# Three matrix exponentials in step: one signal and one predicated copy for each round of squarings

## The chip, the core and the metric

The kernel runs on one core of one Trainium2 chip. The engines of the core are TensorE (PE: matmuls, with PEld for its weight loads), VectorE (DVE), ScalarE (ACT), GpSimd (POOL) and SyncE (SP, which only issues transfers here). The metric is the device time of one execution in microseconds (us); lower is better. Engines run their own instruction streams in order and wait for one another on semaphores.

## What is computed

The reference is a macaron block over x of 8 x 512 x 128: half a feed-forward layer, attention with 16 heads, and half of the same feed-forward layer again. The feed-forward layer normalises x, computes a dense branch, sends each row to 2 of 8 experts, and rotates the expert output by the exponentials of three 128 x 128 generators:

```python
for i in range(NROT):                       # NROT = 3
    moe_out = moe_out @ expm(gens[i])
combined = jnp.concatenate([abel_out, moe_out], axis=-1)
gate = jax.nn.sigmoid(combined @ gc_w + gc_b)
mixed = abel_out * (1.0 - gate) + moe_out * gate
```

## The kernel before

The kernel has no scheduler: each engine's program is written out by hand in the order in which it runs, and semaphores are waited for by value. It has four stages. In the opening stage (to about 149 us of the profile) the rows of all 8 batches ("chunks", numbered n or g) are normalised and routed, POOL scatters them to their experts' regions in DRAM, and beside it the weights are prepared. Then come the experts of the first layer, the attention of 8 batches, and the experts of the second layer.

The weight preparation is where the change lies. The product of the three exponentials is multiplied into the experts' second weights once (`w2_rot`), so the first expert matmul waits for it (`w_ready`). Each exponential is a Taylor series of a scaled generator, squared up to SQUARINGS = 18 times. All 18 rounds are always run. `mats` holds for each generator r the matrix and its transpose side by side (`exp_m`, `exp_T`, 2 x 128 columns). In round i PE makes both squares of each generator into a PSUM bank of that generator, `banks[r]`, and DVE copies them over the matrices where the mask `over[:, r, i]` is set. The semaphore `square_pe` counts PE's finished generators and `squared` counts DVE's finished copies, so before the change PE may square generator 0 of the next round while DVE still copies generators 1 and 2.

The rounds are spread over the routing of chunks n = 2 to 7, three to a chunk; the text calls them A, B and C.

- On DVE, for each n: `gate_logits` (L1633) and `gate_top` (L1645 to L1661, ends with the tile `chosen`), copies of round A, `gate_place` (L1670 to L1685), `gate_shift` (L1628), copies of rounds B and C. After C of n = 2 stands `small_parts` (L1456), after C of n = 3 `make_table` (L1722 to L1751).
- On PE, for each n: `transpose_z(n+1)` (L2197), squares A (L2125 and L2126), `ranks(n)` (L2226 to L2231, which waits for `chosen`), squares B, `abel_logits(n+1)` (L2213 and L2214), squares C, `transpose_w2` (L2112; L2118 for n = 6).
- For n = 7 there are no `abel_logits` and no transposes, so A, B and C are parted by `ranks` alone.

After the last round `fold_rotation` multiplies the three exponentials together (L2132, L2134), makes the rotated weights (L2136, 16 products at L2143) and copies them to `w2_rot` on DVE (L1578). The experts' first PE instruction stands at L2246.

The function `mm` is PE's matmul. An fp32 matmul appears in the profile as two passes, and so does its weight load.

Of the kernel before, what the change touches and what calls it, by code (L numbers as in the profile page):

```python
# [12 lines left out]
U32 = mybir.dt.uint32  # L13
# [5 lines left out]
P = 128  # L19
# [10 lines left out]
NROT = 3  # L30
# [4 lines left out]
SQUARINGS = 18  # L35
# [141 lines left out]
def macaron_block(nc, x, q_w, q_b, k_w, k_b, v_w, v_b, o_w, o_b, ln_gamma, ln_beta, abel_w, abel_b,  # L177
# [11 lines left out]
    with ctx:  # L189
# [3 lines left out]
        def bank(name, shape=(P, 512), dt=FP32):  # L193
            return ctx.enter_context(nc.psum_tensor(name, list(shape), dt))

        def sem(name):
            return ctx.enter_context(nc.semaphore(name))
# [72 lines left out]
        def piece(*shape):  # L270

            n = int(np.prod(shape))
            ap = arena[:, taken[0]:taken[0] + n]
            taken[0] += n
            assert taken[0] <= 2 * NQ * PT_W
            if len(shape) == 2:
                return ap.rearrange("p (a b) -> p a b", a=shape[0])
            if len(shape) == 3:
                return ap.rearrange("p (a b c) -> p a b c", a=shape[0], b=shape[1])
            return ap  # L280
# [7 lines left out]
        mats = piece(NROT, 2, P)  # L288
        exp_m, exp_T = mats[:, :, 0, :], mats[:, :, 1, :]
# [7 lines left out]
        over, shrink = (piece(NROT, SQUARINGS) for _ in range(2))  # L297
# [89 lines left out]


        pair = bank("pair", (P, 2, 512))
        banks = [bank(f"bank{i}") for i in range(6)] + [pair[:, 0, :], pair[:, 1, :]]  # L390

        ps_x, ps_up, ps_y = banks[2:4], banks[0:2], banks[4:6]

# [32 lines left out]
        horner, squared = sem("horner"), sem("squared")  # L426
# [4 lines left out]
        square_pe = sem("square_pe")  # L431
# [87 lines left out]
        def wait(engine, steps, item, step=None):  # L519
            engine.wait_ge(steps.sem, steps.value(item, step))  # L520
# [875 lines left out]
        def _(dve):  # L1396
            v = nc.vector
# [152 lines left out]
            def keep_squares(rounds):  # L1550

                for i in rounds:
                    for r in range(NROT):
                        dve.wait_ge(square_pe, NROT * i + r + 1)
                        v.copy_predicated(mats[:, r, :, :], over[:, r, i:i + 1].bitcast(U32).unsqueeze(2)
                                          .to_broadcast([P, 2, P]),
                                          banks[r][:, 0:2 * P].rearrange("p (a n) -> p a n", a=2)).then_inc(squared, 1)

            def fold_rotation():
                dve.wait_ge(rot_pe, 1)  # L1560
# [341 lines left out]
            for n in range(2, CH):  # L1902
                gate_logits(n)
                gate_top(n)
                keep_squares(range(3 * n - 6, 3 * n - 5))
                gate_place(n)
                if n + 2 < CH:
                    gate_shift(n + 2)
                keep_squares(range(3 * n - 5, 3 * n - 3))
                if n == 2:  # L1910
                    small_parts()
                if n == 3:
                    make_table(0)
# [142 lines left out]
        def _(pe):  # L2056
            mm = nc.tensor.matmul
# [61 lines left out]

            def square(rounds):  # L2120
                for i in rounds:
                    for r in range(NROT):

                        pe.wait_ge(squared, NROT * (i - 1) + r + 2 if i else 1)
                        mm(banks[r][:, 0:P], exp_T[:, r, :], exp_m[:, r, :], start=True, stop=True)  # L2125
                        mm(banks[r][:, P:2 * P], exp_m[:, r, :], exp_T[:, r, :], start=True,  # L2126
                           stop=True).then_inc(square_pe, 1)

            def fold_rotation():
                pe.wait_ge(squared, 1 + NROT * SQUARINGS)  # L2130
                pe.wait_ge(w2T_ok, 5)
                mm(banks[3][:, 0:P], exp_T[:, 1, :], exp_m[:, 2, :], start=True, stop=True).then_inc(rot_pe, 1)  # L2132
                pe.wait_ge(rot_ok, 1)
                mm(banks[3][:, P:2 * P], exp_T[:, 0, :], rot[:, 0, :], start=True, stop=True).then_inc(rot_pe, 1)  # L2134
                pe.wait_ge(rot_ok, 2)
                mm(banks[3][:, 2 * P:2 * P + ROW], b2_T, rot_x, start=True, stop=True).then_inc(rot_pe, 1)  # L2136
                wait(pe, xn_ok, CH - 1)
                wait(pe, placed, CH - 1, 5)
                for q in range(6):
                    if q == 3:  # L2140
                        pe.wait_ge(bias_parts, 1)
                    for i in range(3 * q, min(3 * q + 3, E * NJ)):
                        last = mm(banks[q][:, ROW * (i - 3 * q):ROW * (i - 3 * q + 1)], w2_T[:, i // NJ, i % NJ, :], rot_x,  # L2143
                                  start=True, stop=True)
                    last.then_inc(rot_pe, 1)
# [185 lines left out]
            for n in range(2, CH):  # L2331
                if n + 1 < CH:
                    transpose_z(n + 1)
                square(range(3 * n - 6, 3 * n - 5))
                ranks(n)
                square(range(3 * n - 5, 3 * n - 4))
                if n + 1 < CH:
                    abel_logits(n + 1)
                square(range(3 * n - 4, 3 * n - 3))
                if n - 2 < E // 2:  # L2340
                    transpose_w2(n - 2)
                if n == 6:
                    transpose_b2()
            fold_rotation()

            def scores_for_max(b, u, n):
# [266 lines left out]
```

## Time and profile before

| what | value |
|---|---|
| time, median of 3 executions | 788.86 us (786.06 to 794.77) |
| profiled execution, first to last instruction | 883.8 us |
| mean granted TensorE clock in it | 0.913 of full |
| granted clock from 60 to 150 us of it | 0.78 of full |
| PE busy, DVE busy over the span | 77%, 64% |

The only time of the profiled execution that is at hand is its span, 883.8 us, which is 94.9 us over the median of the executions without a profile. Positions such as "at 91.4 us" are counted from the first instruction of the profiled execution. A row of the timeline gives start, length, engine, line, operation, destination<-sources, shape, count, and in brackets how long the engine had been idle and what ended that; "remote" there, and "another core or an unknown queue" in the chain of waits, mean that no releasing instruction is seen at the end of the wait.

### The profile page before, as it was taken

How to read it: one execution, taken by the hardware profiler on the slowest of the kernel's cores; microseconds unless marked ns; L12 is line 12 of the kernel's file. 1: busy time of each engine (PE TensorE's matmuls, PEld its weight loads, DVE VectorE, ACT ScalarE, POOL GpSimd, SP SyncE). 2: the span in 40 equal slices, each digit the busy share in tenths (PEclk: the TensorE clock that was granted, in tenths of full speed). 3: DMA queues.
4: the chain of work that ended last, by engine and by line, in shares of the span. 5: the costliest groups of instructions: out<-in, count | busy, mean ns of one | idle time of the engine just before them, and what ended most of it. 6: DMA issues, size and time to landing. Idle time of an engine off the chain costs nothing.

```text
span 883.8 us, 16149 instructions
## 1 busy us (share of the span) xinstructions
PE 683.1 (77%) x4719; PEld 492.3 (56%) x4719; DVE 568.2 (64%) x1922; ACT 410.8 (46%) x931; POOL 485.6 (55%) x588
## 2 busy tenths in 40 slices
PE   1465667979897798997988979999997777838760
PEld 1355656979793354654646545455544466837750
DVE  3675545968767876876767767787673235745538
ACT  2243411545560265664545645556554655615530
POOL 2656554034512666576866768373645466566661
PEclk9968777988898899998999999999997999969985
DMA  8614544744348313023050240302201235233525
GB/s 242 205 48 117 132 123 115 183 112 105 94 113 192 110 31 98 18 65 87 2 130 21 49 103 1 98 17 55 61 13 53 85 78 167 75 93 84 175 96 154
DMA packets 89825, 84.04 MB, mean 95 GB/s; under 512 B 14561, under 2 KB 72556, under 8 KB 89580
## 3 DMA queue, kind: packets, MB, share of 16 engines
q1 hardware_dynamic: 74472, 57.51, 25.8%
q0 software_dynamic: 8800, 19.72, 7.5%
q10 hardware_dynamic: 6468, 5.79, 2.8%
q8 instruction: 40, 0.66, 0.3%
q14 instruction: 45, 0.37, 0.1%
HBM read 43.84 MB, written 31.13 MB: 85 GB/s over the span
## 4 chain that ended last, share of the span: by engine, by line
PE 46%; DVE 15%; another core or an unknown queue 11%; issue 7%; ACT 7%; SPq 5%; ACTq 3%; DMA 3%; POOL 1%; DVEq 0%; POOLq 0%
PE bank L2361 6%; PE bank L2271 6%; PE bank L2401 6%; PE bank L2286 6%; PE bank L2426 6%; SPq L595 4%; DVE mx_of L1923 3%; PE pair L2449 2%; PE bank L2363 2%; ACT beside_parts L1254 2%; DMA qT<-mT_zero 2%; PE pair L2213 2%; PE bank L2246 1%; ACT arena L1326 1%
## 5 line engine op out<-in xcount | busy, mean ns | idle before, releaser
L1326 ACT ACTIVATE arena<-bank 128x512 f32<-128x512 f32 x320 | 184.0, 599 | 175.2 <-PE bank L2401 147.1
L1923 DVE TENSOR_REDUCE mx_of<-bank 128x4 f32<-128x512 f32 x320 | 204.2, 684 | 81.9 <-PE bank L2361 42.9
L2401 PE MATMUL bank<-qT,kZ 128*128 128x512 f32 (+3 forms) x512 | 156.9, 377 | 19.2 <-ACT arena L1326 12.4
L975 POOL TENSOR_SCALAR_AFFINE_SELECT arena<-arena 128x256 f32<-128x256 f32 (+1 forms) x192 | 95.4, 521 | 123.9 <-ACT arena L1326 122.5
L2361 PE MATMUL bank<-kZ,qT 128*128 128x512 f32 x320 | 148.5, 481 | 15.7 <-DVE mx_of L1923 6.2
L2401 PEld LDWEIGHTS bank<-qT,kZ 128*128 128x128 f32 x512 | 95.7, 197 | 49.2 <-ACT arena L1326 24.1
L868 POOL DMA_INDIRECT z_rows<-beside_kZ,place x80 | 78.7, 984 | 51.5 <-DVE place L1685 29.8
L2361 PEld LDWEIGHTS bank<-kZ,qT 128*128 128x128 f32 x320 | 63.1, 200 | 70.7 <-issue 31.4
L885 POOL DMA_INDIRECT sums<-y_rows,y_place x56 | 54.4, 971 | 84.9 <-DMA y_rows<-arena 70.0
L2426 PE MATMUL bank<-arena,vA 128*9 128x512 f32 (+3 forms) x1024 | 92.4, 440 | 5.2 <-POOL arena L975 2.7
L1254 ACT ACTIVATE beside_parts<-bank,hidden_bias 128x128 f32<-128x128 f32 x160 | 45.5, 381 | 69.6 <-remote 44.0
L2286 PE MATMUL bank<-w_rot,beside_parts 128*128 x320 | 51.2, 297 | 31.7 <-ACT beside_parts L1254 29.0
L1254 ACT ACTIVATE arena<-bank,hidden_bias 128x128 f32<-128x128 f32 x160 | 45.5, 371 | 48.7 <-PE bank L2271 33.4
L1799 DVE TENSOR_SCALAR arena<-bank,arena 128x132 f32<-128x132 f32 x128 | 39.3, 348 | 44.3 <-remote 25.1
L944 POOL DMA_INDIRECT y_rows<-arena x48 | 49.3, 1026 | 31.8 <-DVE arena L1799 20.5
L2286 PEld LDWEIGHTS bank<-w_rot,beside_parts 128*128 128x128 f32 x320 | 43.9, 197 | 36.2 <-issue 35.3
L2286 PE MATMUL bank<-w_rot,arena 128*128 x320 | 50.4, 295 | 7.0 <-issue 5.2
L868 POOL DMA_INDIRECT z_rows<-w,place x48 | 47.0, 979 | 13.4 <-issue 13.4
L2271 PE MATMUL bank<-beside_parts,beside_qT 128*128 128x128 f32 x320 | 46.6, 286 | 8.3 <-issue 5.1
L2363 PE MATMUL bank<-fixed,ident_bf 128*128 128x512 bf16 x128 | 52.5, 410 | 0.0
L2271 PE MATMUL bank<-arena 128*128 128x128 f32 x320 | 47.0, 291 | 3.8 <-DVE arena L1846 2.2
L2286 PEld LDWEIGHTS bank<-w_rot,arena 128*128 128x128 f32 x320 | 44.6, 200 | 9.0 <-issue 8.2
(286 smaller groups left out, 1306.7 us busy)
## 6 DMA issues: line engine op xcount, KB each, us to landing
arena<-z_rows SPq DMA_DIRECT2D x128, 66.0 KB
qT<-parts SPq DMA_DIRECT2D x42, 128.0 KB
kZ<-parts SPq DMA_DIRECT2D x168, 32.0 KB
y_rows<-arena SPq DMA_DIRECT2D x20, 264.0 KB, 3.3
kZ<-bias_k_r SPq DMA_DIRECT2D x8, 512.0 KB
beside_kZ<-y_rows SPq DMA_DIRECT2D x7, 528.0 KB, 3.9
z_rows<-in_spare SPq DMA_DIRECT2D x4, 528.0 KB
z_rows<-in_spare SPq DMA_DIRECT2D x32, 66.0 KB
```

The lines of the kernel that those rows point to most:

```text
L868: g_.indirect_dma_start(z_rows[run], bass.IndirectOffsetOnAxis(place[g % DEEP][:, k, t:t + 1], 0), zz(g)[:, k, t, :], None).then_inc(z_sen ...
L885: g_.indirect_dma_start(terms(0, c)[0][:, t, k, :], None, y_rows[run], bass.IndirectOffsetOnAxis(y_place[:, c, k, t:t + 1], 0)).then_inc(s ...
L975: g_.affine_select(out=cut, in_=cut, compare_op=ALU.is_ge, fill=0.0, base=0, pattern=[[0, 2], [0, blocks], [1, P]], channel_multiplier=-1) ...
L1254: a_(hidden_rows(layer, p)[:, i, j, :], ps_up[p % 2][:, P * n:P * (n + 1)], ACT.Gelu, bias=hidden_bias[:, j, bass.ds(e, 1)]).then_inc(hidd ...
L1326: a_(dst, src, ACT.Exp).then_inc(exp_ok.sem, 1)
L1923: v.tensor_reduce(mx_of[:, queries, :, t, keys], ps_a[n % NA][:, :].rearrange("p (q n) -> p q n", q=NQ), AX.X, ALU.max).then_inc(reduced.s ...
L2271: last = mm(into, tile(w1_e, j), tile(turned_x(layer, q), t), start=True, stop=True)
L2286: mm(into, hidden_rows(layer, p)[:, i, j, :], w2_rot[:, bass.ds(e, 1), j, :].rearrange("p a n -> p (a n)"), start=(j == 0), stop=False)
L2361: last = mm(into, qT[u][:, t, P * queries:P * (queries + 1)], heads, start=True, stop=(queries != keys))
L2363: last = mm(into, ident_bf[:, :], mask_qk[:, :].unsqueeze(1).to_broadcast([P, NQ, P]), start=False, stop=True)
L2401: return mm(outp, kZ[u][:, h, lo:lo + P], qT[u][:, t, lo:SEQ], start=start, stop=True, skip_group_check=(kind != "full"))
L2426: last = mm(ps_o[32 * q:32 * q + HD + 1, kb * P:SEQ], vA[u][:, kb, NG * q + t, :], pT[t % 2][:, q, PT_KB[kb]:PT_KB[kb] + n], start=(kb == ...
```

## The change

The three banks of the generators become one PSUM tensor `trio` of 3 x 512 columns. A round's six products stand in the same order, but PE waits once before them and signals once after the last, and DVE takes all three results with one predicated copy of 128 x 768. The counts that are waited for follow.

```diff
         pair = bank("pair", (P, 2, 512))
-        banks = [bank(f"bank{i}") for i in range(6)] + [pair[:, 0, :], pair[:, 1, :]]
+        trio = bank("trio", (P, NROT, 512))
+        banks = [trio[:, r, :] for r in range(NROT)] + [bank(f"bank{i}") for i in range(NROT, 6)]
+        banks += [pair[:, 0, :], pair[:, 1, :]]
...
                 for i in rounds:
-                    for r in range(NROT):
-                        dve.wait_ge(square_pe, NROT * i + r + 1)
-                        v.copy_predicated(mats[:, r, :, :], over[:, r, i:i + 1].bitcast(U32).unsqueeze(2)
-                                          .to_broadcast([P, 2, P]),
-                                          banks[r][:, 0:2 * P].rearrange("p (a n) -> p a n", a=2)).then_inc(squared, 1)
+                    dve.wait_ge(square_pe, i + 1)
+                    v.copy_predicated(mats.rearrange("p r a n -> p r (a n)"),
+                                      over[:, :, i:i + 1].bitcast(U32).to_broadcast([P, NROT, 2 * P]),
+                                      trio[:, :, 0:2 * P]).then_inc(squared, 1)
...
                 for i in rounds:
+                    pe.wait_ge(squared, i + 1)
                     for r in range(NROT):
-
-                        pe.wait_ge(squared, NROT * (i - 1) + r + 2 if i else 1)
                         mm(banks[r][:, 0:P], exp_T[:, r, :], exp_m[:, r, :], start=True, stop=True)
-                        mm(banks[r][:, P:2 * P], exp_m[:, r, :], exp_T[:, r, :], start=True,
-                           stop=True).then_inc(square_pe, 1)
+                        last = mm(banks[r][:, P:2 * P], exp_m[:, r, :], exp_T[:, r, :], start=True, stop=True)
+                    last.then_inc(square_pe, 1)
 
             def fold_rotation():
-                pe.wait_ge(squared, 1 + NROT * SQUARINGS)
+                pe.wait_ge(squared, 1 + SQUARINGS)
```

On DVE, at the end of the last chunk (n = 7), the rows before the change are these; `x6` are the copies of rounds B and C, and L1561 is the first copy of `fold_rotation`:

```order
L1681 TENSOR_REDUCE place_of<-pick 128x8 [waits placed]
L1685 CAST place<-place_of 128x8 [waits placed]
L1555 COPY_PREDICATED arena<-arena,bank 128x256 [waits square_pe] x6
L1561 COPY oT<-bank 128x128 [waits rot_pe]
L1563 COPY arena<-bank 128x128 [waits rot_pe]
```

and after it these:

```order
L1682 TENSOR_REDUCE place_of<-pick 128x8 [waits placed]
L1686 CAST place<-place_of 128x8 [waits placed]
L1556 COPY_PREDICATED arena<-arena,trio 128x768 [waits square_pe] x2
L1562 COPY oT<-bank 128x128 [waits rot_pe]
L1564 COPY arena<-bank 128x128 [waits rot_pe]
```

Nothing moved past anything; six copies of 256 columns, each with its own wait, became two of 768. Over the whole program DVE's 54 copies become 18.

On PE, where round B of a chunk ends in `abel_logits` of the next one, before the change (L2226 to L2231 are `ranks`):

```order
L2231 MATMUL bank<-chosen,fixed 128x8 x4
L2125 MATMUL bank<-arena 128x128 [waits squared]
L2126 MATMUL bank<-arena 128x128
L2125 MATMUL bank<-arena 128x128 [waits squared]
L2126 MATMUL bank<-arena 128x128
L2125 MATMUL bank<-arena 128x128 [waits squared]
L2126 MATMUL bank<-arena 128x128
L2213 MATMUL pair<-gate_w,work 128x136 [waits abel_biased,routed,xn_ok]
```

and after it:

```order
L2231 MATMUL bank<-chosen,fixed 128x8 x4
L2125 MATMUL trio<-arena 128x128 [waits squared]
L2126 MATMUL trio<-arena 128x128
L2125 MATMUL trio<-arena 128x128
L2126 MATMUL trio<-arena 128x128
L2125 MATMUL trio<-arena 128x128
L2126 MATMUL trio<-arena 128x128
L2213 MATMUL pair<-gate_w,work 128x136 [waits abel_biased,routed,xn_ok]
```

The order of PE's products is the same, and its three waits became one ahead of the first product.

## Rows read from the trace of the kernel before

**Rows 1.** The page: span, and busy time of each engine.

```profile
span 883.8 us, 16149 instructions
PE 683.1 (77%) x4719; PEld 492.3 (56%) x4719; DVE 568.2 (64%) x1922; ACT 410.8 (46%) x931; POOL 485.6 (55%) x588
```

**Rows 2.** Chain of waits, 129 to 150 us: start us, length us, what.

```profile
138.41 0.45 DVE arena L1555
138.91 0.57 PE bank L2132 x2
...
141.60 5.07 PE bank L2143 x32
...
149.06 1.06 PE bank L2246 x5
```

**Rows 3.** Groups by form, 60 to 150 us: busy us, mean ns, idle before.

```profile
L1555 DVE COPY_PREDICATED arena<-arena,bank 128x256 f32<-128x256 uint32 x54 | 22.1, 440 | 30.3 <-remote 13.4 <-PE bank L2126 11.5 <-issue 5.2
L1578 DVE COPY w_rot<-bank 128x396 f32<-128x396 f32 x5 | 2.7, 566 | 2.5 <-issue 1.5 <-PE bank L2143 0.9
...
L2125 PE MATMUL bank<-arena 128*128 128x128 f32 x108 | 27.6, 345 | 15.3 <-DVE arena L1555 10.7 <-issue 4.7
```

**Rows 4.** Timeline of DVE, chunk n = 4 and the start of n = 5.

```profile
90.90 1.10 DVE L1555 COPY_PREDICATED arena<-arena,bank 128x256 f32<-128x256 uint32 x3
...
94.37 0.45 DVE L1555 COPY_PREDICATED arena<-arena,bank 128x256 f32<-128x256 uint32 x1 [0.41 <-issue]
96.43 0.89 DVE L1555 COPY_PREDICATED arena<-arena,bank 128x256 f32<-128x256 uint32 x2 [1.62 <-PE bank L2126]
97.61 0.45 DVE L1555 COPY_PREDICATED arena<-arena,bank 128x256 f32<-128x256 uint32 x1 [0.28 <-PE bank L2126]
97.94 0.18 DVE L1633 COPY logit<-pair 128x32 f32<-128x32 f32 x1
...
100.10 0.19 DVE L1661 TENSOR_TENSOR chosen<-pick_of 128x32 bf16<-128x32 f32 x1
```

**Rows 5.** Timeline of PE, the same chunk.

```profile
91.04 0.21 PE L2226 MATMUL bank<-chosen,fixed 128*128 128x32 bf16 x1 [5.37 <-DVE chosen L1661]
...
91.40 0.80 PE L2125 MATMUL bank<-arena 128*128 128x128 f32 x2
...
93.69 0.63 PE L2126 MATMUL bank<-arena 128*128 128x128 f32 x2
94.12 0.66 PE L2213 MATMUL pair<-gate_w,work 128*128 128x136 f32 x2
...
95.73 0.44 PE L2125 MATMUL bank<-arena 128*128 128x128 f32 x2
...
96.90 0.39 PE L2126 MATMUL bank<-arena 128*128 128x128 f32 x2
```

**Rows 6.** Timeline of DVE: copies that started long after PE's products.

```profile
76.90 1.10 DVE L1555 COPY_PREDICATED arena<-arena,bank 128x256 f32<-128x256 uint32 x3 [4.41 <-remote]
...
104.80 1.10 DVE L1555 COPY_PREDICATED arena<-arena,bank 128x256 f32<-128x256 uint32 x3 [4.51 <-remote]
...
110.83 0.44 DVE L1555 COPY_PREDICATED arena<-arena,bank 128x256 f32<-128x256 uint32 x1 [2.12 <-PE bank L2126]
112.97 0.44 DVE L1555 COPY_PREDICATED arena<-arena,bank 128x256 f32<-128x256 uint32 x1 [1.70 <-PE bank L2126]
...
115.13 0.44 DVE L1555 COPY_PREDICATED arena<-arena,bank 128x256 f32<-128x256 uint32 x1 [1.73 <-PE bank L2126]
...
129.18 0.43 DVE L1555 COPY_PREDICATED arena<-arena,bank 128x256 f32<-128x256 uint32 x1
132.01 0.44 DVE L1555 COPY_PREDICATED arena<-arena,bank 128x256 f32<-128x256 uint32 x1 [2.40 <-remote]
133.48 0.44 DVE L1555 COPY_PREDICATED arena<-arena,bank 128x256 f32<-128x256 uint32 x1 [1.03 <-remote]
```

**Rows 7.** Timeline of DVE, after the last round: a smaller copy from PSUM.

```profile
139.50 0.29 DVE L1561 COPY oT<-bank 128x128 f32<-128x128 f32 x1 [0.65 <-PE bank L2132]
```

**Rows 8.** One stretch: length, busy us of each engine, granted clock, DMA share, GB/s.

```profile
60.00:150.00 90.00, 57.66 (x410) 52.99 (x409) 48.20 (x246) 23.07 (x55) 49.55 (x49) 0.78 0.50 125
```

## The prediction

> **What bounds the kernel now.** I read the page first [rows 1]: PE is busy for 77% of the span and DVE for 64%, so neither sets the time by its sum, and what a change is worth has to be read in its own stage. The squarings all lie between 61 and 139 us. So I took the chain of waits there next [rows 2]. The reader should see one unbroken line: the last predicated copy (138.41 us), 0.04 us later the first product of the fold (138.91), the rotated weights (L2143), their copies to SBUF (L1578), and the experts' first transposes at 149.06 us. Everything after 149 us waits for the squarings to end, and the experts and the attention are long PE-bound stages behind it. I therefore pass a delay or a gain of the last copy to the end one for one.
>
> Third, the groups by form [rows 3]: 54 copies of 440 ns, with 30.3 us of idle time before them, and PE idle for 15.3 us before its squares, 10.7 of them for the copies. Here two engines hand each other work and both wait; neither is saturated. What counts is the length of the round trip, not the number of instructions.
>
> **What a copy costs.** The 54 small copies become 18 of 128 x 768, a form the trace lacks. A copy from PSUM of 128 columns takes 0.29 us [rows 7] and one of 396 takes 0.566 us [rows 3]: 0.276 us for 268 columns, 1.03 ns a column. The predicated copy of 256 takes 0.440 us [rows 3]; 512 columns more add 0.53 us, which makes 0.97 us. Bounds: not under 0.86 us, if only 0.83 ns a column were added, and not over the 1.10 us that three chained small ones take from first start to last end [rows 4]. I take 0.97 us, since the slope comes from the same kind of access. For DVE alone this is a gain of 0.13 us a round where all three products lie ready, 18 x 0.13 = 2.3 us of its time.
>
> **What a hand-over costs.** Before, PE starts the next round when the first generator's copy has ended, 0.44 us after the copies start; now it waits for all three. Likewise the last generator's copy started when its own product was done and ended 0.44 us later; now the 0.97 us copy starts there. Each time the round trip grows by 0.97 - 0.44 = 0.53 us, if PE waits for DVE there and nothing else does the waiting. Chunk n = 4 shows the three kinds [rows 4, 5].
>
> - A to B: the copies start at 90.90 us, with no idle time before them. PE's B starts at 91.40 us, behind the first copy; the new copy ends at 90.90 + 0.97 = 91.87 us, so B starts at about 91.93 us, 0.53 us late. There are 6 of these, one a chunk: 6 x 0.53 = 3.2 us. Queued behind on PE are `abel_logits` and C, which are late by the same.
> - B to C: between them PE has the logits, 94.12 to 95.73 us, 1.6 us. The last copy of B starts at 94.37 us; the new one would start 0.53 us later, at 94.90 us, and end at 95.87 us, while PE, also 0.53 us late, asks for it at 96.26 us. Hidden, with 0.4 us to spare, for n = 2 to 6: cost 0. If that cover were gone each would cost up to 0.53 us, 2.7 us in all.
> - C to the next chunk: DVE's next routing step stands behind the last copy of C in the queue. That copy ran from 97.61 us, and the logits' copy followed at 97.94 us; with B's delay the new copy starts at 98.14 us and the logits' copy follows at about 99.0 us: 1.06 us late, of which 0.53 us is new. PE's A of the next chunk is also late by this, but it runs beside DVE's routing, 2.3 us from the logits' copy to the end of `chosen` at 100.29 us, and it takes 1.4 us at the clock of round C [rows 5]. Who waits is PE's `ranks` and then B, behind `chosen`. 5 times 0.53 = 2.7 us.
> - The last chunk has no logits between B and C and no routing behind C: two more hand-overs with no cover, 1.1 us. There the fold waits at once [rows 2].
>
> The sum is 13 x 0.53 = 6.9 us, with nothing on the other side: the 0.13 us that a finished set of copies saves is spent ahead of `gate_place`, which is off the path while PE's B is later than it. The bank tensor itself costs nothing, since the same banks are used by the same instructions; fewer waits on DVE cost nothing either.
>
> **What the stalls take out of it.** This stage has longer waits than the round trip. At 76.90 and 104.80 us the copies of A began after 4.4 and 4.5 us of idle time that ends in nothing visible; at 110.83, 112.97 and 115.13 us the three copies of one round came 2.1 us apart; and 132.01 and 133.48 us follow 129.18 us in the same way [rows 6]. If such a wait ends at a time that something else sets, a chunk that arrives 1.06 us late loses nothing in front of it. Counting only what lies behind the last stall, the price is three hand-overs of n = 7, 1.6 us; with no stall at all it is 6.9 us. The profiled execution took 95 us more than the median without a profile, so I take its stalls to be longer than in the timed runs but not absent, and stand in the middle: 4.2 us. The sum is made against the profile's own 883.8 us, which would become 888; it lies 94.9 us over the median of 788.86 us, and since the price is in copy durations and not in a share of the span, the same 4.2 us go on the median: **793 us**.
>
> **A rule against the change.** The rows show DVE idle for 30.3 us before these copies [rows 3]. The Trainium skill, page "Perfetto Trace Analysis", section "Optimizing Scalar/DVE Operations", says that grouping into larger operations helps throughput when the engine is saturated, and that where Scalar or Vector are not saturated but cause bubbles elsewhere, breaking instructions up may let work finish sooner. By that rule the change goes the wrong way here, which is the sign that I forecast; read as if DVE were saturated, it would promise 2.3 us of gain instead. The Trainium skill, page "VectorE: DVE Perf Modes", section "The TRN2 errata — SBUF-src ops pay a fixed extra latency per instruction", gives 120 + columns cycles at 0.96 GHz for a VectorE operation from PSUM; my estimate from it is 0.39 us for 256 columns (the trace says 0.44) and 0.93 us for 768, 0.53 us more, and so the same sum.
>
> **Rivals.**
>
> - *The signals are what is slow, and there are fewer of them* (faster). The copies at 110.83, 112.97 and 115.13 us look like a queue of PE's signals that is served one every 2.1 us while transfers are heavy [rows 6]. If each signal pays, one per round comes at the time of the first: 115.13 - 110.83 = 4.3 us gained there and 133.48 - 129.18 = 4.3 us in the last chunk. With the hand-overs paid in full, 6.9 - 8.6 = -1.7 us; if the 4.4 us stalls shrink by half too, -6 us: 783 to 787 us. Against it: at 76.90 and 104.80 us three copies ran back to back after the stall, so there the three signals came at once, and the last is what one signal would wait for.
> - *The clock falls with the added idle time* (slower). PE's 12 passes of a round take 2.7 us in B of n = 4 (91.40 to 94.12) and 1.4 us in C (95.73 to 97.1) [rows 5]: the same passes at 1.2 and at 2.4 GHz, and over the stretch the granted clock is 0.78 [rows 8]. B came after PE had stood idle for 5.4 us waiting for `chosen` [rows 5]. If half a microsecond of more idle time at each hand-over keeps PE at 1.2 GHz for one more round in a chunk, that is 1.3 us x 6 = 8 us on top of up to 6.9 us, 797 to 804 us. It decides from the point where 0.5 us more of idle time suffices. Against it: the long idle times are there already, and C came back to full clock within the same chunk.
> - *The stalls cover everything, or the large copy is nearly as quick as the small one*: no change, 788 to 790 us. For it speaks that 13.4 us of the idle time ends at no visible releaser [rows 3].
> - *The change does not do what it says* can be left aside: the order of instructions shows 18 copies and one wait a round.
>
> **How the numbers follow.** 1% is 7.9 us, about what a measurement of this kernel can tell from no change. The forecast (+1.6 to +6.9 us, 790.5 to 795.8) gets 0.58; no change (788 to 790.5) 0.14; the signals (783 to 787) 0.14, a third of it under 781; the clock (797 to 804) 0.14. Of the forecast's and the no-change case's chance a little goes past the bounds, because the median of three executions itself ranged from 786.06 to 794.77 us. The range of 784 to 800 us leaves out the lower part of the signals' case and the upper part of the clock's. Faster by over 1% (under 781.0): 0.05. Slower by over 1% (over 796.8): 0.14. Within 1%: 0.81.
>
> **What would show it.** In the profile after, the copy of 128 x 768 should take 0.93 to 1.0 us and stand 18 times; PE's B should start about 1.0 us after the copy of A starts; the last copy should end about 1 us before the fold's other steps as now, but later than the products by 0.97 instead of 0.44 us. The experts' first instruction should come 1.6 to 7 us later than at 149.06 us if the stalls stay as they are. Copies that start right after PE's products, with the stalls gone [rows 6], would speak for the signals. A granted clock in 60 to 150 us clearly under 0.78 [rows 8] would speak for the clock. I would be wrong altogether if the stage's length moved by more than 8 us: then the stalls, not the copies, are what the change moves.

## The result, and the profile after

| | before | after |
|---|---|---|
| time, median of 4 executions each, on one chip | 788.52 us (786.06 to 794.77) | 800.37 us (797.14 to 802.89) |
| ratio, with its 95% interval | | 1.0142 (1.0108 to 1.0176) |
| profiled execution | 883.8 us, and 786.2 us in a second one | 795.4 us |

The changed kernel is slower by 1.4%, 11.2 us, with an interval of 8.5 to 13.9 us. The forecast was slower by 4.2 us with bounds of 1.6 to 6.9 us: its direction held and its size did not. The median lies 0.4 us above the upper end of the range that was given (784 to 800 us).

The first thing to settle was what to compare with. The profile of before that the prediction rests on lasted 883.8 us, against 788 us for the executions that were only timed. So the same kernel was profiled once more, and that execution ("the second profile of before" from here on) took 786.2 us. The top of its page answers to [rows 1]:

```profile
span 786.2 us, 16149 instructions
PE 651.7 (83%) x4719; PEld 471.6 (60%) x4719; DVE 565.6 (72%) x1922; ACT 410.9 (52%) x931; POOL 484.8 (62%) x588
```

The page of the changed kernel begins:

```profile
span 795.4 us, 16113 instructions
PE 654.0 (82%) x4719; PEld 473.9 (60%) x4719; DVE 560.5 (70%) x1886; ACT 412.4 (52%) x931; POOL 485.7 (61%) x588
```

DVE has 36 instructions fewer and 5.1 us less work (565.6 to 560.5), and PE's work is the same within 2.3 us. The span is 9.2 us longer. The change takes work from an engine and lengthens the kernel, so the time must be in waits.

The groups by form answer to [rows 3]. In the second profile of before, over 60 to 140 us (busy us, mean ns of one, idle us ahead and what ended it; the first three of its 54 copies lie before 60 us):

```profile
L2125 PE MATMUL bank<-arena 128*128 128x128 f32 x99 | 20.6, 290 | 0.5 <-DVE arena L1555 0.5
L1555 DVE COPY_PREDICATED arena<-arena,bank 128x256 f32<-128x256 uint32 x51 | 20.2, 440 | 5.1 <-PE bank L2126 4.3 <-issue 0.7
```

and in the changed kernel over the same stretch:

```profile
L2125 PE MATMUL trio<-arena 128*128 128x128 f32 x102 | 22.5, 305 | 6.4 <-DVE arena L1556 6.4
...
L1556 DVE COPY_PREDICATED arena<-arena,trio 128x768 f32<-128x768 uint32 x18 | 18.2, 1012 | 17.0 <-PE trio L2126 17.0
```

The reader should see three things. The idle time ahead of the copies, 30.3 us in [rows 3], was 5.1 us in the second profile of the same kernel, and the 13.4 us that ended at "remote" are not there at all: those stalls belonged to one execution. After the change the idle time is 17.0 us, all of it for PE's products, and PE in turn waits 6.4 us for the copies where it waited 0.5 us. And the copy of 768 columns takes 1.012 us, against 0.97 forecast, while three small ones are 0.440 us each and overlap, so that they take 1.10 us from the first start to the last end.

One chunk shows the round trip. This is DVE's timeline for n = 5 in the second profile of before, which answers to [rows 4] (rows with x3 are the three copies of a round):

```profile
84.65 0.18 DVE L1633 COPY logit<-pair 128x32 f32<-128x32 f32 x1
...
86.94 1.10 DVE L1555 COPY_PREDICATED arena<-arena,bank 128x256 f32<-128x256 uint32 x3
...
89.10 1.10 DVE L1555 COPY_PREDICATED arena<-arena,bank 128x256 f32<-128x256 uint32 x3
90.89 1.34 DVE L1555 COPY_PREDICATED arena<-arena,bank 128x256 f32<-128x256 uint32 x3 [0.69 <-PE bank L2126]
92.13 0.18 DVE L1633 COPY logit<-pair 128x32 f32<-128x32 f32 x1
```

The same chunk on DVE after the change:

```profile
90.78 0.18 DVE L1634 COPY logit<-pair 128x32 f32<-128x32 f32 x1
...
93.01 1.00 DVE L1556 COPY_PREDICATED arena<-arena,trio 128x768 f32<-128x768 uint32 x1
95.71 1.03 DVE L1556 COPY_PREDICATED arena<-arena,trio 128x768 f32<-128x768 uint32 x1 [0.51 <-PE trio L2126]
98.44 1.02 DVE L1556 COPY_PREDICATED arena<-arena,trio 128x768 f32<-128x768 uint32 x1 [1.70 <-PE trio L2126]
99.35 0.17 DVE L1634 COPY logit<-pair 128x32 f32<-128x32 f32 x1
```

And PE's first product of round B, before and then after, which answers to [rows 5]:

```profile
87.43 0.49 PE L2125 MATMUL bank<-arena 128*128 128x128 f32 x2
```

```profile
94.07 0.49 PE L2125 MATMUL trio<-arena 128*128 128x128 f32 x2 [0.56 <-DVE arena L1556]
```

From the start of A's copies to the start of B it was 87.43 - 86.94 = 0.49 us and is 94.07 - 93.01 = 1.06 us: 0.57 us more, the difference of the two copies' lengths (1.012 - 0.440). From one logits' copy to the next the chunk took 92.13 - 84.65 = 7.48 us and takes 99.35 - 90.78 = 8.57 us: 1.09 us more, two hand-overs. The copies of C, which in before began as soon as the first generator's products were there and then went on beside PE, now stand idle for 1.70 us until the last product is done.

The same reading for all chunks (from the start of each logits' copy, us):

| chunk | second profile of before | after | more |
|---|---|---|---|
| n = 2 | 8.12 | 9.27 | 1.15 |
| n = 3 | 10.90 | 13.72 | 2.82 |
| n = 4 | 9.28 | 10.35 | 1.07 |
| n = 5 | 7.48 | 8.57 | 1.09 |
| n = 6 | 7.41 | 8.54 | 1.13 |
| n = 7, to the end of the last copy | 7.11 | 8.63 | 1.52 |

Together 8.8 us. Four chunks have two hand-overs' worth (1.14 us), the last has a little less than the three that the sum gives it (1.7 us), and n = 3 has 1.7 us more than its two, which comes back below as the clock.

Then the chain of waits behind the squarings, which answers to [rows 2]. After the change it reads (start us, length us, what):

```profile
124.05 0.79 DVE w_rot L1579 x2
...
124.89 2.50 issue
127.39 0.64 PE trio L2246 x4
```

In [rows 2] the experts' first transposes come last in an unbroken line behind the rotated weights, and in the second profile of before they follow at once: its weights were ready at 115.2 us and this row of PE's timeline follows (L1403 is the helper by which DVE signals `w_ready`):

```profile
115.31 1.09 PE L2246 MATMUL bank<-ident,arena 128*128 128x128 f32 x8 [0.70 <-DVEq L1403]
```

After the change there are 2.5 us in which PE waits, with the weights ready, for something that the chain doesn't name. So the experts' start moves from 115.31 to 127.39 us, by 12.1 us: 1.1 us by which the squarings began later in that execution (59.7 against 58.6 us), 8.8 us in the squarings, -0.2 us between them and the rotated weights, and 2.4 us more of this wait (2.5 against 0.1).

### The profile page after: what moved, and what is told of

Its sections match the earlier page's. It is cut to its first block, busy times and chain, and to the rows that moved or that the text cites. A ratio compares the mean times of both kernels' runs of the same rounds, so it can differ in the third digit from the quotient of the medians.

```text
span 795.4 us, 16113 instructions
## 1 busy us (share of the span) xinstructions
PE 654.0 (82%) x4719; PEld 473.9 (60%) x4719; DVE 560.5 (70%) x1886; ACT 412.4 (52%) x931; POOL 485.7 (61%) x588
## 4 chain that ended last, share of the span: by engine, by line
PE 51%; DVE 21%; issue 7%; DMA 6%; POOL 5%; ACT 4%; ACTq 3%; SPq 3%; DVEq 0%; POOLq 0%
PE bank L2426 8%; PE trio L2271 6%; PE bank L2286 6%; PE trio L2361 5%; DVE mx_of L1924 4%; PE trio L2401 4%; PE bank L2401 3%; PE bank L2361 3%; PE pair L2213 3%; DMA qT<-mT_zero 2%; POOL y_rows L946 2%; SPq L597 2%; PE pair L2449 2%; DVE arena L1556 2%; PE trio L2363 2%
## 5 line engine op out<-in xcount | busy, mean ns | idle before, releaser
L1924 DVE TENSOR_REDUCE mx_of<-trio 128x4 f32<-128x512 f32 x216 | 142.6, 684 | 40.6 <-PE trio L2361 24.1
L1328 ACT ACTIVATE arena<-trio 128x512 f32<-128x512 f32 x170 | 101.0, 600 | 82.8 <-PE trio L2401 81.9
L1328 ACT ACTIVATE arena<-bank 128x512 f32<-128x512 f32 x150 | 89.6, 597 | 72.2 <-PE bank L2401 71.4
L2361 PE MATMUL trio<-kZ,qT 128*128 128x512 f32 x216 | 99.6, 470 | 6.9 <-DMA kZ<-parts 2.2
L1924 DVE TENSOR_REDUCE mx_of<-bank 128x4 f32<-128x512 f32 x104 | 71.2, 684 | 28.6 <-PE bank L2361 27.2
L2401 PE MATMUL trio<-qT,kZ 128*128 128x512 f32 (+3 forms) x272 | 83.2, 372 | 5.2 <-DMA qT<-mT_zero 5.2
L2401 PE MATMUL bank<-qT,kZ 128*128 128x128 f32 (+2 forms) x240 | 73.2, 366 | 1.0 <-ACT arena L1328 0.2
L2401 PEld LDWEIGHTS trio<-qT,kZ 128*128 128x128 f32 x272 | 49.4, 192 | 20.9 <-DMA qT<-mT_zero 7.3
L2361 PE MATMUL bank<-kZ,qT 128*128 128x512 f32 x104 | 49.0, 471 | 7.6 <-DVE mx_of L1924 4.0
L870 POOL DMA_INDIRECT z_rows<-w,place x48 | 46.9, 976 | 13.4 <-issue 13.4
L2401 PEld LDWEIGHTS bank<-qT,kZ 128*128 128x128 f32 x240 | 45.1, 192 | 13.5 <-ACT arena L1328 8.6
```

Of the source, the lines that this page charges most:

```text
L870: g_.indirect_dma_start(z_rows[run], bass.IndirectOffsetOnAxis(place[g % DEEP][:, k, t:t + 1], 0), zz(g)[:, k, t, :], None).then_inc(z_sen ...
L1328: a_(dst, src, ACT.Exp).then_inc(exp_ok.sem, 1)
L1924: v.tensor_reduce(mx_of[:, queries, :, t, keys], ps_a[n % NA][:, :].rearrange("p (q n) -> p q n", q=NQ), AX.X, ALU.max).then_inc(reduced.s ...
L2361: last = mm(into, qT[u][:, t, P * queries:P * (queries + 1)], heads, start=True, stop=(queries != keys))
L2401: return mm(outp, kZ[u][:, h, lo:lo + P], qT[u][:, t, lo:SEQ], start=start, stop=True, skip_group_check=(kind != "full"))
```

## Experiments

All ratios are to the kernel before, from executions on the same chip and with their 95% intervals. One program serves for most kernels. It has the PSUM tensor `trio` and says with two tables which generators' products signal and which copies are joined. Its difference from before, without the two functions that count up to the right semaphore value:

```diff
-        banks = [bank(f"bank{i}") for i in range(6)] + [pair[:, 0, :], pair[:, 1, :]]
+        trio = bank("trio", (P, NROT, 512))
+        banks = [trio[:, r, :] for r in range(NROT)] + [bank(f"bank{i}") for i in range(NROT, 6)]
+        banks += [pair[:, 0, :], pair[:, 1, :]]
...
-                    for r in range(NROT):
-                        dve.wait_ge(square_pe, NROT * i + r + 1)
...
+                    for lo, hi in COPIES[i]:
+                        dve.wait_ge(square_pe, signals_up_to(i, hi))
+                        v.copy_predicated(mats[:, lo:hi, :, :].rearrange("p r a n -> p r (a n)"),
+                                          over[:, lo:hi, i:i + 1].bitcast(U32).to_broadcast([P, hi - lo, 2 * P]),
+                                          trio[:, lo:hi, 0:2 * P]).then_inc(squared, 1)
...
-                        pe.wait_ge(squared, NROT * (i - 1) + r + 2 if i else 1)
+                        pe.wait_ge(squared, copies_up_to(i - 1, r) if i else 1)
...
+                        if r in SIGNALS[i]:
+                            last.then_inc(square_pe, 1)
```

A round that is "joined" has SIGNALS[i] = [2] and COPIES[i] = [(0, 3)]; one that is "apart" has [0, 1, 2] and [(0, 1), (1, 2), (2, 3)]. The results:

| kernel | ratio | interval | squarings, us | weights ready, us | experts' start, us |
|---|---|---|---|---|---|
| second profile of before | | | 48.1 | 115.2 | 115.31 |
| tensor only | 0.9996 | 0.9962 to 1.0030 | 48.2 | 115.9 | 116.01 |
| one signal, small copies | 1.0127 | 1.0091 to 1.0162 | 54.2 | 120.3 | 126.92 |
| three signals, one copy | 1.0160 | 1.0128 to 1.0192 | 55.6 | 123.1 | 126.53 |
| the change | 1.0142 | 1.0108 to 1.0176 | 56.8 | 124.8 | 127.39 |
| before, biases first | 0.9989 | 0.9963 to 1.0014 | 48.2 | 116.2 | 116.31 |
| one signal, small copies, biases first | 1.0068 | 1.0042 to 1.0094 | 54.2 | 120.8 | 121.37 |
| the change, biases first | 1.0090 | 1.0062 to 1.0119 | 56.8 | 125.3 | 125.45 |
| only rounds A joined, biases first | 1.0014 | 0.9984 to 1.0044 | 52.9 | 120.9 | 121.03 |
| only rounds C joined, biases first | 0.9988 | 0.9955 to 1.0022 | 50.3 | 116.5 | 117.09 |
| only the last two joined, biases first | 1.0001 | 0.9964 to 1.0038 | 49.8 | 118.9 | 119.03 |
| only rounds B joined | 0.9981 | 0.9952 to 1.0009 | 48.7 | 116.2 | 116.84 |
| only rounds B joined, biases first | 0.9974 | 0.9946 to 1.0002 | 48.5 | 116.8 | 116.87 |

"Squarings" is from the start of the first predicated copy to the end of the last, in the kernel's profile. There is one profile for each kernel, so these lengths have no interval of their own.

**Before, once more.** No edit. It tells what the stalls of the first profile are.

> The kernel before once more, for a profile that can be compared with the one after: its first one was 95 us over the timed runs. Hand-over theory (each joined round costs the round trip the large copy's 1.01 us in place of 0.44 us, nothing else changes): the span is about 787 us, the copies of round A start right behind the routing, and the last copy ends about 8 us earlier than in the changed kernel, at about 108.5 us from the first instruction. Rival (something behind the squarings pays too, the attention or the experts): the squarings end less than 8 us earlier and the rest of the 11 us lies behind 150 us.

It took 787.93 us, with a span of 786.2 us. The stalls are gone: the squarings take 48.1 us, not the 75.9 us (63.0 to 138.9) of the first profile. So what is in [rows 6] belongs to that one execution. None of the profiles of the other kernels, with spans of 785 to 799 us, has it either.

**The tensor only.** All rounds apart: three signals and three copies, as before, from the one PSUM tensor.

> Only the PSUM tensor over three banks is kept; three signals and three copies of 256 columns a round as before. Hand-over theory: no change, 787 to 790 us. Rival (the joined tensor, or where the banks lie, costs part of the 11 us): 791 to 795 us.

0.9996 (to within 0.3% on each side) and 48.2 us: no cost of the layout or of the rewritten form of the copy can be seen.

**One signal, small copies.** PE waits for each generator's copy by itself but signals once a round.

```diff
+SIGNALS[i] = [2] in all 18 rounds
+COPIES[i] = [(0, 1), (1, 2), (2, 3)] in all 18 rounds
```

> One signal of TensorE a round, but still three copies of 256 columns, each with a wait of TensorE of its own. Hand-over theory: the copies of A still give the first generator free after 0.44 us, so A to B costs nothing; behind a last product DVE now needs 1.10 us in place of 0.44 us, 0.66 us x 5 chunks and once ahead of the fold, and the uncovered hand-over of the last chunk costs 0.8 us: 4.8 us in all, about 793 us. Rival (signals are dear, fewer are better): 785 us or less.

It was slower than expected: 1.0127, 801.6 us. The squarings took 6.0 us more than with the tensor only. A copy of generator 0 can't start until the last product is done. By chunks, n = 3 alone is 2.70 us longer than with the tensor only, where n = 2, 5 and 6 are 0.56 to 0.67 us longer; some 2.0 us of the 6.0 are therefore the fall of the clock that is told below, and 4.0 us are the hand-overs, which is somewhat less than the 4.8 us expected. The other part of the miss is behind the squarings. The chain of waits there:

```profile
117.61 2.69 DVE w_rot L1596 x6
...
120.36 6.56 issue
126.92 1.09 PE trio L2264 x4
```

The weights are ready at 120.3 us and PE starts 6.6 us later.

**Three signals, one copy.** The reverse.

```diff
+SIGNALS[i] = [0, 1, 2] in all 18 rounds
+COPIES[i] = [(0, 3)] in all 18 rounds
```

> Three signals of TensorE a round as before, but one copy of 768 columns that waits for the third, and one wait of TensorE. Hand-over theory: the same as the whole change, 799 to 801 us, since the copy waits for the last product either way. Rival (fewer signals give something back or cost something): it differs from the whole change by more than 2 us.

1.0160: it has as many signals as before and costs as much as the whole change, so the number of signals has no price that can be seen. It must wait for the last product as well, and adds the long copy. Its squarings are 7.4 us longer than with the tensor only (55.6 against 48.2), which is 13 x 0.57; its n = 3 is 1.2 us longer, without the fall of the clock. After this run the wait of 2.5 to 6.6 us behind the ready weights stood in all three slow kernels, and in neither of the others.

**The wait behind the weights.** PE's code ahead of L2246 names three waits: `w_ready`, `expert_bias_in` (the experts' biases) and `w1_in`. The biases are three loads of 2.1 KB that ScalarE issues when `bias_parts` is set, shortly ahead of the rotated weights. The rows of the timeline on the issues in the changed kernel (start us, us from the first to the last, queue):

```profile
115.36 3.29 SPq L609 DMA_DIRECT2D kZ<-bias_k_r  x3
121.17 2.13 ACTq L1270 DMA_DIRECT2D expert_bias<-arena  x3
```

and in the second profile of before:

```profile
110.95 2.13 ACTq L1268 DMA_DIRECT2D expert_bias<-arena  x3
113.21 0.90 SPq L607 DMA_DIRECT2D kZ<-bias_k_r  x2
```

SyncE's loads of the attention's key rows are 512 KB each and are released by POOL's scatters. In before the small loads go ahead of the last two of them; after the change, with the squarings' end 9.9 us later and chunk 6's scatter only some 5 us (from about 113 to 118 us), they go behind. With one signal and small copies the two queues issue at the same time: the large loads at 118.39 and 118.81 us, the small ones at 117.61, 118.44 and 119.14 us. Their packets, in the groups of transfers by queue (packets, MB, share): for one signal with small copies, first in 117 to 123 us, then in 123 to 127 us:

```profile
q10 hardware_dynamic: 29, 0.00, 0.4%
```

```profile
q10 hardware_dynamic: 19, 0.00, 0.4%
```

In the second profile of before, over 110 to 114.5 us:

```profile
q10 hardware_dynamic: 48, 0.01, 1.0%
```

The same 48 packets took 3.4 us from first issue to last landing (110.95 to 114.3 us) in the one and 9.2 us (117.61 to 126.8 us) in the other, and 6.1 us (121.17 to 127.3 us) in the changed kernel. The times of the last of their semaphore's increments in the traces say that this is what PE waits for: 126.83 us with one signal and small copies, 126.44 us with three signals and one copy, 127.30 us in the change, and in each PE starts 0.09 us later (126.92, 126.53, 127.39 us). In the second profile of before the last increment comes at 114.34 us, ahead of the ready weights at 115.2 us. The test is to hold the large loads back until the small ones have landed:

```diff
             for q in range(X_TOP, X_BUFS):
                 load_x(0, q)
+            sp.wait_ge(expert_bias_in, 16 * 3)
             for g in range(5, CH - 1):
                 key_rows_of(g)
```

It was put into the kernel with one signal and small copies, into the change, and into before as a control.

> One signal a round, three copies, and SyncE waits for the three small loads of the experts' bias rows before it issues the key rows of chunks 5 to 7 (512 KB each). Theory of the overtaken loads (the experts start only when these 2.1 KB loads have landed, and they now come behind the key rows): w_rot is ready at about 120.3 us and the experts start there, not at 126.9 us, so 5 to 6 us less than with one signal alone, a ratio to before of about 1.006. Rival (the experts' start waits for something else, the scatter or the x rows): no change, ratio 1.012 to 1.014.

> The whole change with the same wait of SyncE. Overtaken loads: w_rot is ready at 124.8 us and the experts start at about 125 us, where they started at 127.4 us: 2 to 3 us less than the changed kernel, ratio to before 1.011 to 1.012. What is left is the hand-overs, 8 us. Rival: ratio 1.014 to 1.016 as before.

> The kernel before with the same wait of SyncE. Overtaken loads: there the loads land at 114.3 us, ahead of w_rot at 115.2 us, so nothing is gained: ratio 0.998 to 1.002. Rival (key rows issued later free the transfers for all else): faster by over 3 us.

The chain of waits with one signal, small copies and the biases first:

```profile
120.84 0.53 issue
121.37 0.64 PE trio L2265 x4
```

and its issues, now in the other order:

```profile
118.09 2.13 ACTq L1287 DMA_DIRECT2D expert_bias<-arena  x3
...
121.29 1.41 SPq L625 DMA_DIRECT2D kZ<-bias_k_r  x3
```

The wait behind the weights fell from 6.6 to 0.5 us, and the ratio from 1.0127 to 1.0068. The 0.5 us are still the biases, which now land at 121.28 us, 3.2 us after their first issue. In the change it fell from 2.5 to 0.1 us, and the ratio from 1.0142 to 1.0090 (its interval and the earlier one, 1.0062 to 1.0119 and 1.0108 to 1.0176, still touch). Before gains nothing from the same edit (0.9989), since it had no such wait. So the late biases are shown as a cost of the change. The wait that went is 0.3% of the time and the ratios differ by 0.5%, with an uncertainty of nearly as much. 0.9% remain, 7.6 us (796.69 against 789.11 us for before with the same edit). In the profiles of these two kernels the squarings differ by 8.6 us and the experts' start by 9.1 us, so the squarings are the cause to look at for the rest.

**One kind of round at a time.** The prediction has a term for each kind of hand-over, so each kind was joined alone: rounds B of chunks 2 to 6; rounds A of 2 to 7; rounds C of 2 to 6; and B and C of the last chunk, which have no cover.

```diff
+fused B:    SIGNALS[i] = [2], COPIES[i] = [(0, 3)] for i in (1, 4, 7, 10, 13)
+fused A:    the same for i in (0, 3, 6, 9, 12, 15)
+fused C:    the same for i in (2, 5, 8, 11, 14)
+fused last: the same for i in (16, 17)
```

> One signal and one copy only in rounds B of chunks 2 to 6, where the logits stand between B and C on TensorE; all other rounds as before. Hand-over theory: the copy of B is hidden under the logits, the squarings end where they ended before (106.7 us) within 0.5 us, ratio 0.998 to 1.002. Rival (each joined round costs the same, 0.6 us): the squarings end 3 us later, ratio 1.004 or more.

> With the wait of SyncE for the bias rows, one signal and one copy only in the six rounds A; all others as before. Hand-over theory: TensorE's B starts 0.57 us later in each of six chunks, 3.4 us in all: ratio to before 1.003 to 1.006, and the last predicated copy ends about 3.4 us later after its first one than the 48.1 us of the kernel before. Rival (only the last stretch counts): ratio 0.998 to 1.001.

> The same, joined only in rounds C of chunks 2 to 6. Hand-over theory: the last copy of C ends 0.57 us later in five chunks, and the routing behind it: 2.9 us, ratio 1.002 to 1.005, 2.9 us more than 48.1 us from the first copy to the last. Rival (TensorE's early start of the next round A was what mattered, and it hides behind the routing): ratio 0.998 to 1.001.

> The same, joined only in rounds B and C of the last chunk, where nothing stands between them on TensorE. Hand-over theory with what the profile after showed: in its last chunk the rounds came 2.7 us apart where three copies keep up with TensorE at 1.34 us a round, so B to C costs 1.1 us or somewhat less and C to the fold 0.57 us behind a copy of B that waits for the routing: 1.0 to 1.7 us, ratio 1.000 to 1.003. Rival: nothing.

> Joined only in rounds B of chunks 2 to 6, with the wait of SyncE: what the runs so far leave as the best that can be made of the change. Hand-over theory: no difference that can be told, ratio 0.997 to 1.001. Rival (fewer copies on VectorE give something once nobody waits for them): under 0.996.

In the squarings' length, against 48.2 us of before with the biases first: A 4.7 us, C 2.0 us, the last two 1.5 us, B 0.3 us, together 8.5 us, where the whole change adds 8.6 us. That they meet so closely is in part luck, since chunks in which nothing is joined differ by up to 0.5 us as well: n = 4 takes 9.28 us in the second profile of before and 9.70 us in before with the biases first, and of the 1.5 us of the last two only 1.16 us lie in their own chunk. In their own chunks the kinds read so: A costs 0.55 to 0.58 us in n = 2, 4, 5 and 6, nothing in n = 7 as long as B and C behind it are apart, and 2.47 us in n = 3; C costs 0.56 to 0.62 us in n = 2, 3, 5 and 6 and can't be read in n = 4; the last two cost 1.16 us together, two times 0.58. B costs 0.3 us for five with the biases first and 0.5 us without (48.7 against 48.2 us with the tensor only), nearly all of it in n = 4, so close to nothing, as worked out.

The times are another matter: 1.0014, 0.9988, 1.0001 and 0.9974, all with intervals of 0.3 to 0.4% to each side that hold 1. A's stage is 4.7 us longer, its experts start 4.7 us later, and of this 1.1 us of time was measured, with an interval of -1.3 to 3.5 us. So the lower part of what A alone was expected to cost (1.003 to 1.006) is just within the interval, and the one for one that I had counted on is not. Added up, the four ratios give 2 us less than before, with an uncertainty of about 5 us (my estimate from their intervals), where the whole change with the biases first is 7 us slower. The lengths of the parts add up to the whole and their times do not; no run explains that. The kernel with only B joined and the biases first has the lowest ratio, by medians 790.85 against 791.83 us, and can't be told from before.

## Why the prediction was right or wrong

**The bound was right.** The last copy, the fold, the rotated weights and the experts' start are one line in every kernel. They did not move as one block. From the end of the last copy to the ready weights nine profiles, both kinds of before among them, take 8.3 to 8.5 us at a mean granted clock of 0.79 or 0.80, and four (the two with one signal and small copies, C joined, and B joined without the biases first) take 7.0 us at 1.00. And the experts' biases can come later than the weights.

**The copy was sized nearly right**: 1.012 us against 0.97, so a hand-over costs 0.57 us and not 0.53. That makes the full sum 13 x 0.57 = 7.4 us in place of 6.9. The slope is (1.012 - 0.440) / 512 = 1.12 ns a column; for the 0.83 ns of the lower bound no row stood. The estimate from the Trainium skill, page "VectorE: DVE Perf Modes", section "The TRN2 errata — SBUF-src ops pay a fixed extra latency per instruction", 0.93 us, was further off.

**The count of hand-overs was right,** but for A of n = 7, which costs nothing by itself. A and C cost 1.07 to 1.15 us a chunk in four chunks of five, two times 0.57 and nearly nothing else, and B to C was hidden behind `abel_logits`: 0.3 to 0.5 us for five of them where uncovered ones would have cost 2.9. In the changed kernel's n = 5, B's copy ended at 96.74 us and PE asked for it at 96.83 us, so the spare is about 0.1 us, where 0.4 us was forecast from n = 4 at another clock. The last chunk's three came to 1.5 us, against 3 x 0.57 = 1.7.

**The step that failed is the halving for the stalls.** I took the full sum down from 6.9 to 4.2 us because waits of 2 to 4.5 us stood in [rows 6], and argued that they were "longer than in the timed runs but not absent". They were absent. The profiled execution was 95 us longer than the timed ones, and the second profile of the same kernel has a span within 3 us of the timed median and 5.1 us of idle time ahead of the copies. The full sum, which stood in the text as the upper bound, is what the squarings pay: 7.4 us of the 8.8 us measured, with 1.7 us of the clock beside it and 0.3 us less than the sum in the other chunks. The prediction had said that a stage longer by more than 8 us would mean that the stalls are what the change moves. The stage is 8.8 us longer, and there were no stalls to move: that sign would have misled.

**The clock happened in one place.** The rival put the loss of 1.3 us into every chunk. It came in n = 3 alone. The stretch of n = 3's round B, after the change (length, busy us of PE, PEld, DVE, ACT and POOL, granted clock, DMA share, GB/s):

```profile
70.00:74.00 4.00, 3.99 (x20) 3.84 (x21) 2.00 (x10) 2.87 (x8) 3.08 (x4) 0.57 0.89 254
```

In the second profile of before:

```profile
70.00:74.00 4.00, 3.73 (x34) 3.54 (x32) 3.19 (x12) 2.72 (x7) 3.06 (x4) 1.00 0.79 251
```

Before ran it at full clock (2.4 GHz), after the change it ran largely at the lower level (1.2 GHz), with 20 matmul records in the stretch instead of 34, and the chunk is 2.82 us longer and not 1.1. The same extra stretch is in the kernels with one signal, in the change with the biases first, and in the one with rounds A joined (4.7 us longer, of which 5 x 0.57 = 2.9 us are hand-overs); it is not in the one with rounds C joined, and also not in the one with three signals and one copy, though its B starts as late. So a later B doesn't suffice, and what makes the clock fall there stays open: no run changed the idle time alone. It is worth 1.7 us once in the change (1.9 us with rounds A joined, 2.0 us with one signal), where the rival had 8 us. The measured 800.37 us lies within that rival's 797 to 804 us by coincidence, since 2.4 us of the 11.2 us come from the biases, which no rival had. The page over 60 to 120 us has a granted clock of 0.94 before and 0.90 after.

**The rival of the signals is refuted**: three signals with one copy cost as much as one signal with one copy, and one signal by itself is a loss.

**What no step had** is the second wait at the experts' start. I treated the rotated weights as the only thing that PE waits for there, because in [rows 2] they come last. The late squarings put the bias loads among or behind the large ones, and this added 2.4 us. It is not a cost of the squarings themselves but of small loads that are in flight together with large ones.

**One for one to the end** held roughly for the whole change: the experts' start is 12.1 us later (11.0 us by the distance from the first copy), the span 9.2 us and the time, by its ratio, 11.2 us. It did not hold for the small parts (A: 4.7 us later, 1.1 us of time measured). C's stage is 2.0 us longer and its experts start 0.8 us later than before's, because its fold ran at full clock: 7.0 us in place of 8.5, with 0.5 us of waiting for the biases behind it. From the experts' start to the end the thirteen profiles take 668.0 to 674.0 us, in no order that goes with how late the start was (before 670.9, before with biases first 673.1, the change 668.0, A alone 669.3). So single profiles can't tell whether a later stage gives a few microseconds back, and it stays open.

**Behind the rule against the change** the runs stand plainly. The Trainium skill, page "Perfetto Trace Analysis", section "Optimizing Scalar/DVE Operations", says that smaller instructions may let work finish sooner where DVE is not saturated but causes bubbles elsewhere. Here DVE shed 5.1 us of work by the larger copies and the kernel became 11 us longer.

## What to carry to other kernels

Where two engines hand a loop's state back and forth, a larger instruction saves its fixed cost and charges the difference between the whole copy and the first piece (here 0.57 us) at each hand-over that nothing covers, and joining the signals alone lengthened the squarings by 6.0 us where the whole change took 8.8: count the uncovered hand-overs first. Where the other engine has work of its own in between, as here between B and C, joining is free and brings next to nothing. If the profiled execution is much longer than the timed ones, take a second profile before any wait in it is given a price; and when a stage gets later, look at every wait in front of the next one, since small loads may now be in flight together with large ones.

## What was unexpected of the hardware

- One profiled execution of before took 883.8 us and another 786.2 us. The difference in the squarings (75.9 against 48.1 us) was in waits that end at nothing visible and in a granted clock of 0.78 from 60 to 150 us [rows 8].
- Three loads of 2.1 KB on ScalarE's queue took 3.4 us to land when they were issued ahead of 512 KB loads on SyncE's queue, 6.1 us when all three came behind three such loads, and 9.2 us when both queues issued at the same time. At the time of the 9.2 us, 19 of their 48 packets were still to come 5.4 us after the first was issued.
- The granted clock of n = 3's round B went from 1.00 to 0.57 with hand-overs that are 0.57 us longer, and did not do so in the four chunks behind it by any amount that their lengths show.
- The same fold and rotated weights, 38 matmul records of PE each time, took 7.0 us at a granted clock of 1.00 in four profiles and 8.3 to 8.5 us at 0.79 or 0.80 in nine. The two kernels with only B joined fell on different sides (7.0 and 8.5 us).
